# A graph layer on one core: the order of VectorE's seven steps in a group of 512 edges

## The reference

```python
h = max(layernorm(x), 0)                       # per node
l0, l1 = x0 @ W_l1_0, x1 @ W_l1_1              # scaled by the node's value: the table
w = relu(radial @ W_fc1 * c) * c' @ W_fc2 * c" # 192 weights per edge: w0 w1 w2 w3
y0, y1 = l0[src], l1[src]                      # gathered rows, 160 floats an edge
m0 = w0 * y0 * e0
m1 = (w1 * y0)[:, :, None] * e1[:, None, :]
m2 = (w2 * e0)[:, :, None] * y1
m3 = w3 * einsum('eud,ed->eu', y1, e1)         # dot product over the axis d
s0..s3 = segment_sum(m0..m3, dst)
out = x + self-products(h) + 0.5 * (s @ W_l2)
```

## Time and profile before

| | |
|---|---|
| runs shown | 2948.76, 2910.21, 2946.77 us; median 2946.77 |
| profiled execution | 2931.67 us, span 2929.9 us |
| PE busy | 2518.0 us, 86% of the span |
| PEld busy | 2003.8 us, 68% |
| VectorE busy | 1661.1 us, 57% |
| ScalarE busy | 340.0 us, 12% |
| GpSimd busy | 1617.6 us, 55% |
| mean granted TensorE clock | 0.749 |

### The profile page before, as it was taken

The page is one execution under the profiler, slowest core; times in us unless marked ns, Lnnn a source line. Parts: engine busy times, 40 slices in busy tenths (PEclk is TensorE's granted clock), DMA queues, the critical chain, the costliest instruction groups (busy, mean ns, idle before and its releaser), DMA issues.

```text
span 2929.9 us, 41982 instructions
## 1 busy us (share of the span) xinstructions
PE 2518.0 (86%) x11466; PEld 2003.8 (68%) x11466; DVE 1661.1 (57%) x4639; ACT 340.0 (12%) x636; POOL 1617.6 (55%) x1637
## 2 busy tenths in 40 slices
PE   6889888788989988888888888898888889898888
PEld 6667776667767766666666666676676677676677
DVE  5455656556656556555655555565565556556555
ACT  5000111011101011010101101010110111011111
POOL 4645555555655555545555554555465555555553
PEclk8566778787767687877777777777778777677876
DMA  4212222222222222212222221222122222222221
GB/s 132 58 45 52 54 55 54 51 53 53 56 50 55 53 52 56 52 47 55 50 53 50 54 55 48 52 51 56 46 60 51 50 52 54 50 55 52 51 53 36
DMA packets 160622, 158.30 MB, mean 54 GB/s; under 512 B 87570, under 2 KB 132534, under 8 KB 160602
## 3 DMA queue, kind: packets, MB, share of 16 engines
q0 software_dynamic: 77376, 132.16, 18.3%
q1 hardware_dynamic: 82088, 24.49, 3.7%
q10 hardware_dynamic: 1138, 1.43, 0.1%
HBM read 149.90 MB, written 8.03 MB: 54 GB/s over the span
## 4 chain that ended last, share of the span: by engine, by line
PE 57%; another core or an unknown queue 15%; DVE 13%; issue 10%; DVEq 4%; ACT 1%; DMA 0%; POOL 0%; ACTq 0%; SPq 0%; POOLq 0%
PE ps_w L894 16%; PE ps_s L922 14%; PE ps_s L924 12%; PE ps_h L887 11%; DVE hot L686 3%; DVEq L745 2%; DVE acc L742 2%; DVE dot L661 2%; DVE dots L656 2%; DVE msg L677 1%; DVE hot L680 1%; PE ps_s L910 1%; DVEq L742 1%; PE ps_s L906 1%
## 5 line engine op out<-in xcount | busy, mean ns | idle before, releaser
L381 POOL DMA_INDIRECT y<-table,idx x1612 | 1583.6, 982 | 1274.2 <-DVE msg L677 657.4
L894 PEld LDWEIGHTS ps_w<-w_fc,hr 100*128 100x128 f32 x3224 | 682.8, 241 | 456.9 <-issue 404.2
L894 PE MATMUL ps_w<-w_fc,hr 100*128 100x192 f32 x3224 | 839.2, 417 | 49.2 <-issue 26.8
L922 PE MATMUL ps_s<-hot,msg 128*128 128x128 f32 x3216 | 612.8, 346 | 136.5 <-DVE msg L677 84.9
L922 PEld LDWEIGHTS ps_s<-hot,msg 128*128 128x128 f32 x3216 | 569.3, 255 | 180.6 <-DVE msg L677 111.8
L742 DVE TENSOR_TENSOR acc<-acc,ps_s 64x32 f32 (+1 forms) x1612 | 327.1, 203 | 628.8 <-remote 346.7
L887 PE MATMUL ps_h<-rad,w_fc 10*100 10x512 f32 x806 | 556.8, 775 | 80.0 <-ACT hid_t L492 43.4
L924 PE MATMUL ps_s<-hot,msg 128*128 128x64 f32 x3216 | 531.6, 314 | 88.1 <-issue 87.7
L924 PEld LDWEIGHTS ps_s<-hot,msg 128*128 128x128 f32 x3216 | 521.0, 241 | 94.6 <-issue 94.2
L487 ACT ACTIVATE hr<-ps_h 100x512 f32<-100x512 f32 x403 | 239.3, 597 | 2409.4 <-remote 1012.6
L667 DVE TENSOR_TENSOR msg<-ps_w,y 128x512 f32<-128x512 f32 x404 | 278.9, 690 | 340.9 <-remote 163.9
(11 more groups left out here) (83 smaller groups left out, 537.4 us busy)
## 6 DMA issues: line engine op xcount, KB each, us to landing
y<-table,idx POOLq DMA_INDIRECT x1612
rad<-in_radial SPq DMA_DIRECT2D x202, 40.0 KB
xres<-in_x SPq DMA_DIRECT2D x7, 560.0 KB, 4.7
out<-xres SPq DMA_DIRECT2D x49, 80.0 KB
table<-y SPq DMA_DIRECT2D x6, 560.0 KB, 3.2
idx<-in_src SPq DMA_DIRECT2D x202, 4.0 KB
attr_sb<-in_attr SPq DMA_DIRECT2D x202, 16.0 KB
dst_i<-in_dst ACTq DMA_DIRECT2D x1, 808.0 KB, 7.2
```

Source lines behind the costliest of these rows:

```text
L381: nc.gpsimd.indirect_dma_start(out=y[:, j, t, :], out_offset=None, in_=table, in_offset=bass.IndirectOffsetOnAxis(ap=idx[:, j // HALF, col ...
L894: ins = nc.tensor.matmul(ps_w[:, s, t, 0:NW], hr[:, s, t * P:(t + 1) * P], w_fc2[:, :], start=True, stop=True)
L922: nc.tensor.matmul(ps_s[:, s, 0:4 * W], msg[:, s, t, 0:P], hot[:, s, t, 1:V, :], start=(t == 0), stop=(t == T - 1))
```

## The change

Within `messages`, VectorE's seven steps come in another order: before comparison, dots, weighing, axis sum, scalar products, vector products, dot products; now dots, comparison, scalar products, weighing, axis sum, vector products, dot products. The wait for `fc2_done` moves with the scalar products, so the weighing and the axis sum now stand behind it; the wait for the gather now stands ahead of the comparison. No instruction is added or removed.

```diff
                 if j % HALF == 0:
                     dve.wait_ge(ld_attr[j // HALF], i * 16 + 16)
-                which(g, s)
                 dve.wait_ge(gathered[j], i * (16 * T) + 16 * T)
                 edge_dots(j)
+                which(g, s)
+                dve.wait_ge(fc2_done, g + 1)
+                scalar_products(j, s)
                 weigh(g, j, s)
                 dve.wait_ge(dots_done, g + 1)
                 sum_dots()
-                dve.wait_ge(fc2_done, g + 1)
-                scalar_products(j, s)
                 vector_products(j, s)
```

## The result

The kernel with the change takes 2989.45 us (median of 6 runs, 2970.15 to 2999.26); beside it the kernel before took 2947.77 us (6 runs, 2910.21 to 2956.69). The ratio is 1.0167, with a 95% interval of 1.0099 to 1.0234: 1.7% slower, or 41.7 us between the medians. The profiled execution took 2976.9 us, 45.2 us more than that of before.

What follows compares the result with a forecast made beforehand. TensorE was taken to set the pace in some stretches, late signals during back-to-back gathers in others. 2931.67 us profiled + 46 (late steps) + 0.6 (comparison) = 2978 us, range 2890 to 3035 us.

Steps and rivals of the forecast that it cites:

- The sum: Whole kernel: profiled 2931.67 us plus 46 us and 0.6 us gives 2978 us.
- The late steps (b): After late `fc2` signals, weighing and axis sum delay TensorE's windows by up to 1.22 us in 40 groups: 46 us.
- The hand-overs at 0: Between VectorE's reordered instructions: hand-overs stay the same, taken as 0; 0.05 us a group would be 20 us.
- The comparison behind the dots at 0.6 us at most: VectorE's comparison now waits for the gather too; that wait was 10.6 us in all, so at most 0.6 us.
- The signs: Idle ahead of L667 450 to 530 us, TensorE's L677 waits up 46 us; unchanged VectorE busy time, gather waits, clock.
- The loss is swallowed: Rival: gather bursts decide when frozen stretches end, so TensorE's later entry costs nothing; 2915 to 2950 us, chance 0.26.
- The clock pays too: Rival: longer TensorE stalls lower the granted clock by 0.02, adding about 67 us; 3005 to 3080 us, chance 0.18.
- Fewer stretches: Rival: later gather releases part bursts, so fewer late signals before VectorE's additions; 2840 to 2915 us, chance 0.11.

Runs made afterwards that it cites:

- experiment 8: The change with the window-base register load issued between weighing and axis sum, chip with late signals: 2889.19 us against 2825.34 us for the kernel before, ratio 1.0183.
- experiment 5: The unedited change against the kernel before, on a chip without late signals: 2123.11 us against 2115.73 us, ratio 1.0032.
- experiment 7: `fc2` issued after the windows, one gather in four: order of before 2801.4 us; order of the change, base load between weighing and axis sum, 3601.67 us.
- experiment 2: Kernel before, with the window-base register load held back until the scalar products are done, against the kernel before: 2120.54 us, ratio 1.0001.
- thin gathers: Only one of a group's four gathers issued in the loop: order of before 1890.32 us, the change 1946.99 us, the change with its base load covered 1892.72 us.
- experiment 3: Kernel before with only dots and comparison swapped, against the kernel before: 2181.02 us, ratio 1.0301.
- experiment 1: The change with the window-base register load issued between weighing and axis sum, no late signals: 2124.01 us against 2118.75 us for the kernel before, ratio 1.0031.
- experiment 4: Kernel before with dots and axis sum of the next group moved ahead of the additions, against the kernel before: 2224.22 us, ratio 1.0484.

## Why the prediction was right

**The sum.** Predicted 2978 us (range 2890 to 3035), measured 2989 us. As a difference to the kernel before: 46 us predicted on the profiled execution, 41.7 us between the medians, 45.2 us between the profiled executions. The interval of the ratio (29 to 69 us) is too wide to check the term more closely than that. That the sizes agree so well is in part luck: between the two traces three things moved that the sum had at 0, each of about the size of the term or more: the additions' waits for "issue" (76.8 us more), their waits for "remote" (99.1 us less) and the gathers' busy time (30.9 us less). How much of each was on the path isn't known.

**The late steps (b)** were the right mechanism. In the main result the loss is TensorE's idle time at an unchanged clock, and its matmuls wait 43.6 us more for L677, beside the 46 us predicted. Three experiments agree: with the load covered a loss stays (experiment 8, where the clock may carry a part); where no signal is late the change costs 0.3% (experiment 5); with `fc2` late on purpose the same two steps cost much (experiment 7, mostly through the clock). There are 36 groups in which VectorE waited ahead of L667 and the windows start within 0.1 us of the end of L677, before and after alike (34 of those before had waited for 1.22 us or more, as the prediction counted). The price of one is 1.10 us, not 1.22; 36 x 1.10 = 40 us.

What was not tried where signals are late is each half of the change alone: the dots ahead of the comparison, and the wait for `fc2` ahead of the weighing. For the second speaks that the first leaves no mark in the trace of the changed kernel: the gather is waited for 12.4 us (before 10.6), and the gathers are shorter and not longer.

**The hand-overs at 0** were wrong as a step, though not for the sum. I had looked at VectorE's instructions and their semaphores, and not at what its queue does between them: the load of the base was covered by three products, and the change left it two. The gapless group went from 4.10 to 4.55 us, where I had allowed 0.05 us. Without late signals and behind full gathers it costs nothing (experiment 2), behind thin gathers 57 us; what it cost in the main result isn't shown. The trace of before could have told: the additions waited for "issue" ten times only, which is a cover and not an absence. Nor does a hand-over follow the length of the first instruction alone: from the start of the axis sum it is 0.62 us to the scalar products and 0.50 us to the vector products. In both traces the scalar products start 0.03 us after the instruction before them has ended, while the vector products start before it has.

**The comparison behind the dots at 0.6 us at most** isn't contradicted by the main result (1.8 us more of waits for the gather) and failed as a rule: alone and on a chip where gathers set the pace it costs 3.0%, by way of longer gathers (experiment 3). In the full change the gathers stay short there (experiment 5: 57 of 1612 over 1.1 us; dots first: 276), and the whole change costs 0.3%. That isn't the load, which costs the same 0.3% when it is covered (experiment 1); what it is stays open.

**The signs.** Idle time ahead of L667 went from 333 to 388 us, in 154 groups as before, and not to 450 to 530 us in more groups: I had added VectorE's 1.22 us to each wait, but VectorE comes 0.35 us later with the additions. With the load covered it is 511 us in 196 groups (experiment 8, on another chip). The waits of the additions put down to "remote" fell from 346.7 to 247.6 us, by 29%; far fewer of them was one of the signs of being wrong, and they are 256.0 us in the second trace with the late steps too (experiment 8). TensorE's weight loads wait 32.7 us more for L677, not 46. The clock, the gathers' waits (12.4 us) and VectorE's busy time came as said.

**The rivals.** "The loss is swallowed" is out by the interval, which begins at 1.0099. "The clock pays too" is out for the main result (0.747 against 0.749 in the profiled executions, and no more busy time of TensorE), though not for experiment 8, and experiment 7 shows that mechanism when stalls are in most groups. "Fewer stretches" isn't borne out as a gain: the time rose; whether the 99 us fewer of "remote" ahead of the additions are a small gain that hides a larger loss is open. So is what makes signals late on some chips.

## What to carry to other kernels

A wait that is moved ahead of independent work costs where it ends last; count the groups in which the engine waits there and its consumer then waits for it, and multiply by the work that now comes after, which here gave 46 us for 42. List what an engine's queue does between instructions too, register loads above all, and name what covers each. And look whether the bound is the same on another chip before one order is called better: here the same two kernels differ by 1.7% where signals come late and by 0.3% where gathers set the pace. Before an instruction of VectorE is moved on a chip where gathers are the bound, look which instruction runs at the moment a gather starts.

## What the runs showed of the hardware

The kernel before took 2116 to 2123 us on three chips, 2825 us on a fourth and 2948 us in the main result. In the last two TensorE's signals reached VectorE and ScalarE late while gathers were issued back to back: an `fc2` that ended at 1623.16 let VectorE go on at 1626.11, and single waits of VectorE's additions were up to 11.8 us long. The waits put down to "remote" ahead of the additions ended 1.6 us (trace of before) and 1.8 us (changed kernel) after the end of the last gather that had started, as a median, and a fifth to a quarter of them while a gather was still running. With one gather in four and `fc2` last the trace on such a chip (experiment 7, order of before) has two waits put down to "remote", 25.6 us in all; the trace of before has 76 ahead of the additions alone. So the gathers seem to have a part in it; how is open.

An indirect gather of GpSimd lasts 0.946 us, or up to 1.47 us when it starts while VectorE runs one of three instructions: the comparison (L680), the dots (L656) or the weighing (L686). In the 14 traces, from 100 us on, 1207 gathers of 16309 are longer than 1.05 us. All 1207 started while one of these three was running and had 0.22 us or more to go, and each ended 0.81 to 0.83 us after it. Of the gathers that started at any other time none was longer than 0.963 us, also not those that started during the axis sum or the three products. The three have in common that both their inputs lie in SBUF; the axis sum has one input, and the products and the additions read one from PSUM. A gather isn't lengthened by such an instruction that began less than 0.05 us before it: all 173 gathers that had 0.2 us or more of one beside them at their start and stayed short are of this kind. VectorE, which starts with the landing of a gather, then meets it at the same place in every group: 0.18 us more on the third gather (experiment 3) and 0.28 us on the fourth (experiment 4), times 403 groups, are 3.5 and 5.3% of the time, of which 3.0 and 4.8% were measured.

With TensorE waiting for L677 in 304 groups, 0.59 us as a median, the granted clock was 0.526 over a whole execution, nearly always the level of 1.2 GHz; with 209 such waits of 0.42 us it was 0.744 (experiment 7).
